# Attention steps reordered: VectorE's output product moved behind the subtraction of the row maximum

## The reference

```
def attn(a):                       # once along rows (j), once along columns (i)
    q, (k, v) = ln(a, ga, ba) @ Wq, split(ln(a, gb, bb) @ Wkv)
    q, k = rope(q), rope(k)        # rotary embedding of each 16-wide head
    attn = softmax(q @ k.T)        # 4 heads, rows of 64 scores
    return elu(concat(attn @ v) @ Wo + bo)
x = x + (attn_i(x) + attn_j(x)) / 2
x = z + ff(mamba2(ln(z)));  out = x + mlp(ln(x))      # z is the x of the line above
```

## Time and profile before

| | us |
|---|---|
| median of 3 runs (326.32 to 327.53) | 327.38 |
| the profiled execution | 327.32 |
| its span | 325.2 |
| PE busy | 236.3 |
| DVE busy | 206.1 |
| ACT busy | 173.1 |
| POOL busy | 126.1 |

### The profile page before, as it was taken

The page is one execution under the profiler, slowest core; times in us unless marked ns, Lnnn a source line. Parts: engine busy times, 40 slices in busy tenths (PEclk is TensorE's granted clock), DMA queues, the critical chain, the costliest instruction groups (busy, mean ns, idle before and its releaser), DMA issues.

```text
span 325.2 us, 7775 instructions
## 1 busy us (share of the span) xinstructions
PE 236.3 (73%) x3138; PEld 141.6 (44%) x3138; DVE 206.1 (63%) x333; ACT 173.1 (53%) x298; POOL 126.1 (39%) x104
## 2 busy tenths in 40 slices
PE   0386977958676865754865799997999848956764
PEld 0153644545444443533565165643544424434331
DVE  2696885828474755754374796999767965483422
ACT  2253655637574757446535844566557337723380
POOL 2416364405444242710040494754796832300000
PEclk9999978969997999795596999998999989997555
DMA  7611010243213133304045300000000000011002
GB/s 179 229 67 65 34 35 33 76 105 84 56 43 67 35 67 81 83 3 85 11 94 112 75 2 2 2 3 3 2 2 2 2 0 2 2 39 29 1 0 65
DMA packets 34243, 15.26 MB, mean 47 GB/s; under 512 B 31008, under 2 KB 31520, under 8 KB 34080
## 3 DMA queue, kind: packets, MB, share of 16 engines
q1 hardware_dynamic: 32480, 13.67, 16.7%
q10 hardware_dynamic: 1728, 1.10, 1.4%
HBM read 5.42 MB, written 2.10 MB: 23 GB/s over the span
## 4 chain that ended last, share of the span: by engine, by line
PE 36%; DVE 31%; ACT 16%; issue 13%; DMA 2%; ACTq 1%; DVEq 0%
PE ring L560 14%; PE score L560 9%; DVE s_max L1043 5%; PE ring L565 5%; DVE s_cen L1047 3%; PE p_turn L560 3%; PE oz L560 2%; DVE mix L1134 2%; DVE ln_s L837 2%; DVE rot_sin L1000 2%; DMA back<-x 2%; DVE rot_cos L1000 2%; DVE ln_v L857 2%; DVE xhat L872 2%; ACT wo_b L1250 2%
## 5 line engine op out<-in xcount | busy, mean ns | idle before, releaser
L1520 POOL TENSOR_TENSOR a_msk<-dt_fin,c_sb 128x512 f32<-128x512 f32 x32 | 40.0, 1251 | 25.0 <-DVE dt_fin L975 15.2
L1043 DVE TENSOR_REDUCE s_max<-score 128x16 f32<-128x1024 f32 x16 | 19.6, 1223 | 26.6 <-PE score L560 26.6
L1134 DVE TENSOR_TENSOR mix<-dec,g_m 128x512 f32<-128x512 f32 x32 | 31.5, 988 | 2.2 <-ACT dec L1377 1.5
L1295 ACT ACTIVATE prob_t<-p_turn 128x512 f32<-128x512 f32 x32 | 17.5, 592 | 25.2 <-PE p_turn L565 25.2
L880 POOL TENSOR_TENSOR k_rot<-rot_cos,rot_swap 128x512 f32<-128x512 f32 x7 | 8.9, 1270 | 43.3 <-DMA rot_swap<-rot_sin 39.0
L1505 POOL TENSOR_TENSOR dtx<-xv,dt_fin 64x512 f32<-64x512 f32 x16 | 19.8, 1240 | 13.2 <-PE p_turn L560 12.3
L1303 ACT ACTIVATE prob<-s_cen 128x1024 f32<-128x1024 f32 x16 | 16.9, 1057 | 13.9 <-DVE s_cen L1047 13.8
L560 PE MATMUL score<-a_msk,c_sb 128*128 128x512 f32 x44 | 24.3, 634 | 0.0
L560 PE MATMUL score<-k_bd,q_rot 32*64 32x128 f32 x512 | 22.9, 329 | 0.0
L560 PEld LDWEIGHTS p_turn<-mix,dtx 128*32 128x32 f32 x512 | 11.0, 109 | 27.4 <-issue 14.6
L892 POOL TENSOR_SCALAR k_bd<-k_rot,c_sb 128x512 f32<-128x512 f32 x14 | 22.1, 1588 | 0.7
(11 more groups left out here) (177 smaller groups left out, 567.8 us busy)
## 6 DMA issues: line engine op xcount, KB each, us to landing
rot_swap<-rot_sin SPq DMA_DIRECT2D x32, 128.0 KB, 2.1
p_sb<-params SPq DMA_DIRECT2D x1, 1520.0 KB, 9.7
x_tok<-x SPq DMA_DIRECT2D x16, 64.0 KB
attention_j_turned<-y_tok SPq DMA_DIRECT2D x16, 64.0 KB, 2.2
back<-attention_j_turned SPq DMA_DIRECT2D x16, 64.0 KB, 2.5
ut_a<-u SPq DMA_DIRECT2D x8, 126.0 KB, 2.8
ut_b<-u SPq DMA_DIRECT2D x8, 124.0 KB, 3.1
ut_b<-u SPq DMA_DIRECT2D x8, 122.0 KB, 3.2
```

The source lines that it names most:

```text
L1043: v.tensor_reduce(s_max[:, n % 2, :], sc, AX, ALU.max).then_inc(s_maxed, 1)
L1134: v.tensor_tensor(mix[:, e % LAPS, :, :], dec[:, e % LAPS, :, :], wide(g_m[:, e // 4 % 2, e % 4, :], SSM_H), ALU.mult)\
L1295: a.activation(prob_t[:, e % 2, 4 * hp:4 * hp + 4, :].rearrange("p k n -> p (k n)"), PT[hp], ACT.Identity)\
L1520: gp.tensor_tensor(a_msk[:, m % LAPS, :, :], deep(dt_fin[:, 0, SSM_H * m:SSM_H * (m + 1)], GRID), wide(cst("tri"), SSM_H), ALU.mult).then_ ...
```

## The change

The table is rewritten. A step has now three slots, (a, b, c): on TensorE slot a stands behind the score, slot b behind the turning of the unit before, and slot c behind its product with v. ScalarE does slots a and b ahead of the exponential of the step, and slot c behind the reciprocal. On VectorE `o_t` of step n is that of unit n-2 instead of n-1 and stands right behind `s_cen`; it was behind the rotations before. `y_t` moves from even to odd steps. `wo` stands in the even steps in place of the odd, `vt` still in the odd ones but right behind the score, `k` in the even ones, `q` in the odd ones, `yt` in the even ones, one step later in the count. There is one step more, the tail's steps move by one to three, and the normalisation of the input at the start is interleaved in another way. SyncE's and GpSimd's code keeps its order but for one memset.

```diff
-ATT_STEPS = 25
+ATT_STEPS = 26
-XT_STEP = (13, 15, 17, 19)
-UT_STEP = (15, 17, 19, 21)
-XP_STEP = (17, 17, 18, 18, 20, 20, 21, 21)
+XT_STEP = (16, 17, 18, 20)
+UT_STEP = (18, 19, 20, 22)
+XP_STEP = (19, 19, 20, 20, 21, 21, 22, 22)
...
-    steps = {-1: [("xr", 0), ("k", 0), ("q", 0), ("xr", 1), ("v", 0), ("vt", 0), ("k", 1)]}
+    steps = {-1: ([("xr", 0), ("k", 0), ("q", 0), ("xr", 1), ("v", 0), ("vt", 0)], [], [])}
...
-        if odd:
-            uses = [("wo", g - 1), ("k", g + 2), ("yt", g - 2), ("vt", g + 1)]
+        if n == 0:
+            a, b, c = [("k", 1)], [], []
+        elif n == 1:
+            a, b, c = [("xr", 2), ("q", 1)], [("v", 1)], [("k", 2), ("xr", 3)]
+        elif n == 2:
+            a, b, c = [("vt", 1), ("q", 2)], [("v", 2)], [("k", 3)]
+        elif odd:
+            a, b, c = [("vt", g + 1)], [("q", g + 2)], []
         else:
-            uses = [("q", g + 1), ("v", g + 1)]
+            a, b, c = [("wo", g - 2)], [("v", g + 1)], [("k", g + 2), ("yt", g - 3)]
...
-DT_STEP = 22
+DT_STEP = 23
...
@@ -722,6 +727,8 @@
+                for use in att_slots[n][0]:
+                    att_use(use)
                 if 1 <= n <= UNITS:
...
-                for use in att_steps[n][:1]:
+                for use in att_slots[n][1]:
                     att_use(use)
...
-                for use in att_steps[n][1:]:
+                for use in att_slots[n][2]:
                     att_use(use)
@@ -906,7 +913,6 @@
-            ln_vector_b(v, 1)
             v.wait_ge(sin_signed, 1)
...
-                if use == ("k", 0):
+                if use == ("q", 0):
+                    ln_vector_b(v, 1)
                     ln_vector_c(v, 1)
-                if use == ("q", 0):
                     v.wait_ge(xa_in[2], 32)
...
-                    ln_vector_b(v, 2)
...
-            ln_vector_c(v, 2)
             for n in range(ATT_STEPS):
...
-                e = n - 1
+                e = n - 2
                 if 0 <= e < UNITS:
...
                 if n == 0:
+                    ln_vector_b(v, 2)
+                    ln_vector_c(v, 2)
                     v.wait_ge(xa_in[3], 32)
                     ln_vector_a(v, 3)
...
-                if not odd and 0 <= g - 2 < ATT_CHUNKS:
+                if odd and 0 <= g - 2 < ATT_CHUNKS:
@@ -1294,8 +1301,10 @@
-                if n % 2 == 0 and 1 <= n // 2 < ATT_CHUNKS:
-                    att_use(("vt", n // 2))
+                for use in att_slots[n][0] + att_slots[n][1]:
+                    att_use(use)
+                if n == 1:
+                    ln_scalar_b(a, 3)
...
-                for use in att_steps[n]:
-                    if use[0] != "vt":
-                        att_use(use)
+                for use in att_slots[n][2]:
+                    att_use(use)
```

More of the change, by code:

```diff
@@ L151, in build @@
     lo, n_cols = offsets(COLS)
-    att_steps = attention_uses()
+    att_slots = attention_uses()
+    att_steps = {n: [use for slot in att_slots[n] for use in slot] for n in att_slots}
     ssm_before, ssm_steps = ssm_uses()
```

48 lines of the change are left out of this document (23 added, 25 removed).

## The result

The new order is slower. Its median is 336.21 us (335.48 to 338.40, 4 runs) beside 327.45 us for the kernel before (326.32 to 329.58, 4 runs) on the same chip: ratio 1.027, 95% interval 1.020 to 1.034. The forecast was 330.3, range 323.5 to 335.5. The direction was right; the size was not, and the time fell just outside the range.

The account below looks back on a forecast made before the run. No engine owned the chain; the middle's even scores were expected to wait for SyncE's queue. Start +0.4, middle +0.8, step 14 to 15 -3.6 and tail +5.5 gave +3.1 us, put at 330.3 us, range 323.5 to 335.5.

Parts of the forecast that it names:

- The main step: Steps 6 to 13: q's swap queues behind y_tok's stores, so the next even score comes 14.6 us after S, an even score's start.
- the size of the pair: Steps 6 to 13: three pairs of 15.8 us at half clock, the first 14.9; 62.3 for four against 61.5 before.
- the third rival: Middle pairs: slow swap of 4.0 us and half clock each time, 17.5 us a pair, 338 us in all; chance 0.10.
- The start: Up to step 6's score: step 2 later at 42.0 us, steps 2 to 5 shorter at 28.3; +0.4 us.
- Steps 14 and 15: Score of step 14 to step 15's maximum: 7.1 us, 6.3 at full clock, 8.0 at half; -3.6 us.
- The tail: Step 15's maximum to softplus: all four quarters now behind step 15, 42.5 us against 37.0 before; +5.5 us.
- step 15's maximum near 140, ahead of before: Sign expected in the trace after: VectorE's maximum of step 15 at 140.4 us, before it was 142.85.
- The scan: From softplus to the end: 145.3 us, taken as unchanged since the change touches only what stands ahead of it.
- the scan behind softplus changes its 145 us: Stated condition, from softplus to the end, under which the prediction would be wrong.

Follow-up runs that it names:

- run 1: New order with both swaps of the rotation issued ahead of the wait for y_t and the stores in SyncE's list: 318.44 us, ratio 0.977 to the kernel before.
- Run 2: New order with SyncE still waiting for y_t first, but the swap of q issued ahead of the stores: 318.59 us, ratio 0.976 to the kernel before.
- Run 6: New order with 9 filler multiplications on TensorE ahead of the wait for q at steps 8, 10, 12 and 14: 333.97 us, ratio 1.013 to the kernel before.
- run 13: New order unchanged, profiled a second time: 336.70 us in one execution.
- Runs 3: New order with k of chunk 1 back at its old place ahead of step 0: 338.07 us, ratio 1.039 to the kernel before.
- 9: New order with q of chunk 1 made in step 0 and quarter 3's scaling right behind its variance: 338.88 us, ratio 1.042 to the kernel before.
- run 8: Kernel of run 1 with the tail's first quarter one step earlier: 316.70 us, ratio 0.965 to the kernel before.
- 10: Kernel of run 1 with the output product ahead of the maximum and the tail's first quarter one step earlier: 312.78 us, ratio 0.963 to the kernel before.
- 7: Kernel of run 1 with the output product of step n ahead of step n's maximum on VectorE: 314.50 us, ratio 0.959 to the kernel before.
- 11: As run 10, with denser tail tables, quarters in steps 15, 16, 18, 19: 314.60 us, ratio 0.969 to the kernel before.
- 12: New order with only the output product ahead of the maximum, SyncE's list as in the new order: 337.80 us, ratio 1.037 to the kernel before.

## Why the prediction missed, by its steps

The deviation in the profiled spans is +11.1 us (336.3 against 325.2), forecast +3.1; in the medians it is +8.8. By stage, in the first profile of each kernel, and in the mean of the three profiles of the new order against the two of the kernel before:

| stage | forecast | measured | mean |
|---|---|---|---|
| start, to step 6's score | +0.4 | +2.8 | +3.1 |
| four pairs | +0.8 | +6.5 | +5.9 |
| step 14 to the maximum of step 15 | -3.6 | -2.6 | -3.1 |
| from there to softplus | +5.5 | +8.5 | +9.1 |
| scan | 0 | -4.1 | -4.9 |

Of the 8.0 us between forecast and profile the pairs hold 5.7, the tail 3.0, the start 2.4 and steps 14 to 15 1.0; the scan takes 4.1 back. Without the scan, for which nothing was forecast, the miss would have been 12.1.

**The main step held.** `y_tok` and its stores stand ahead of q's swap, and each even score waits for that swap. The first pair measured 14.60 us, the 14.6 that was laid out (forecast with a margin, 14.9), with the stores at S+7.8 for 7.9 (the terms given for it add up to 8.0); the 2.21 us wait of `yt` for `wo_b` is gone; and without the hold the pair is 12.0 us (12.1 laid out). At this place the Trainium skill says, on the page "DMA: Bandwidth & Descriptors", section "Anatomy of one DMA — SWDGE (gpsimd) path", that the wait happens on the issuing sequencer and not in the DMA engines. The section is about transfers issued by GpSimd, the sentence about all. For SyncE the trace agrees: q of chunk 5 was ready for its swap at 89.4 and nothing was issued for it until the stores had waited and gone, at 100.09. So does run 1: with the swap ahead of that wait in the list the median is 18 us lower. Run 2 keeps the wait and changes only the order of the issues; it shows that the 2.6 us of the stores' issue, with what hangs on it, is what the even scores feel, and not the wait: 20.7 us against 0.8 for the four.

**The step that failed is the size of the pair**, "three of four pairs at half clock, 14.6 + 1.2 = 15.8", with the swap taken at its lower bound of 2.68. Two terms were too small:

- The swap took 2.73 and 2.78 us in two pairs, and 4.27 and 4.05 in the other two, 3.1 us in all above the value taken. The row at 77.61 in the earlier trace rows had shown 4.05 us, and I set it aside because "stores don't explain" it. They indeed don't, but the delay was real and came back; the third rival named it with 0.10.
- Half clock cost 1.5, 2.6 and 2.6 us a pair (9.38, 10.38 and 10.46 to the stores in place of 7.83), where 1.6 was the full price and 1.2 the mean. Besides the score and `wo`, `p_turn` ran at half clock in two of the three. Run 6 gives 6.8 us for the middle.

Together, 4 x 14.6 + 6.7 + 3.1 = 68.2 us, and 68.0 were measured. Nearest is the third rival (17.5 a pair, 338 us, chance 0.10): the last three pairs took 17.8 on average. But it had the slow swap each time, and only two of four were slow; that its total lies near the 336.2 measured is in part luck, since the start and the tail came out longer and the scan shorter than the layout had them. The weights were an error as well: I argued full against half clock from waits "of the size of the old one", but every even score behind a wait of 2.5 us or more was at half clock in the first profile. In the second profile of the new order (run 13) one with 2.50 and one with 2.57 us of wait was at full clock, so the wait's length alone does not decide.

**The start** was 2.8 us and not 0.4. Step 2 stood at 42.4 as laid out (42.0), so the miss lies in steps 2 to 5: 31.0 us where 28.3 were laid out. `o_t` at step 3 stands behind `late_weights` (51.95 to 54.73, 2.8 us where I had estimated 2) and behind maximum and subtraction; TensorE sat idle 4.04 us for it, not 3, and the score behind it took 1.58 us. Runs 3 and 9 show that it is not the place of k's or q's slot. Over ten profiles with this product behind the subtraction the maximum of step 6 came at 72.9 to 76.3 us, in the four with it ahead at 72.4 to 74.1. It came at 72.0 on average in the two profiles of the kernel before. GpSimd's code at the start moved by more than the memset named ahead of the prediction: its second scaling of weights stands behind the first copy of `xn_i` now (13.75 us in place of 11.10), and no run tests that. So this part is explained only in part; the rest stays open.

**Steps 14 and 15** took 8.17 us at a clock of 0.72, the value that the prediction gave for half clock (8.0).

**The tail** took 45.5 us, above the 43.3 given for half clock in every burst. Counted from the maximum of step 15, `x_tok` of quarter 0 came at +10.1 (8.5 laid out), `xhat` 0 at +16.9 (15.2), `xhat` 1 at +24.3 (21.8), `xhat` 2 at +32.7 (29.5) and `xhat` 3 at +41.7 (37.3), so it was behind the marks laid out from the first quarter on, and by more with each. The sign "step 15's maximum near 140, ahead of before" failed with it: it came at 149.56, behind the 142.85 of before, as the start and the pairs had lost more than these steps gain. The three profiles of the new order agree on the tail (45.4 to 45.5). Tables alone moved it by 1.6 us (run 8 beside 1), 1.1 (10 beside 7) and 4.2 (11 beside 10), over all from 43.6 to 47.8 and never near the 37.0 and 35.7 of before; that the work of all four quarters now stands behind step 15 was argued, and no run put a quarter ahead of step 14 to show it.

**The scan** was taken as fixed and gave 4.1 us back. Nothing of its code changed. Its clock is 0.92 in place of 0.88:

```profile
179.88:325.20 145.32, 117.27 (x1462) 61.56 (x1454) 97.79 (x154) 77.39 (x128) 64.27 (x51) 0.88 0.05 12
```

VectorE, ScalarE and GpSimd are busy about as long as before (98.6, 78.5 and 64.2 us for 97.8, 77.4 and 64.3), TensorE for 4.5 us less. Where TensorE falls to half clock in the scan seems to depend on how the kernel enters it, which was argued and not tested: runs 6, 9 and 12, with the new order's tail and other edits upstream, had 144.7 to 145.6 us. What in the entry decides is open. That "the scan behind softplus changes its 145 us" was among the things that would make the prediction wrong, but no range was given for it; its 4 us alone are more than the whole forecast.
